# Normalised y of a fused state-space and feed-forward block: split token-major and transposed by DMA, the norm's scale and shift moved into the gate's weights and bias, y rebuilt by channel on GpSimd

## The reference

```
z0, x0, xBC, dt = split(layernorm(x) @ W_in.T)
xBC = silu(causal_conv4(xBC) + conv_b);  x, B, C = split(xBC)
h_t = exp(dt*A) h_(t-1) + dt * x_t B_t;  y_t = h_t C_t + D * x_t    (8 heads of 64 channels, 16 states)
y = layernorm(y) * ln_gamma + ln_beta                               (512 channels)
y = sigmoid(y @ W_gate.T + b_gate) * y
x = x + concat(silu(z0) * x0, y) @ W_out.T
h = layernorm(gelu(layernorm(x) @ tern(W_fc).T)) * ln_w + ln_b;  x = x + h @ tern(W_proj).T
```

## Time and profile before

| | |
|---|---|
| runs | 1303.48, 1304.63, 1305.02 us (median 1304.63) |
| profiled execution, its own time | 1306.39 us |
| its span, first to last instruction | 1304.6 us |
| mean granted TensorE clock | 0.962 |
| TensorE busy | 1150.3 us (88%), 8534 matmuls |
| VectorE (DVE) busy | 1061.3 us (81%), 2116 instructions |
| ScalarE (ACT) busy | 929.3 us (71%), 1500 instructions |
| GpSimd (POOL) busy | 348.3 us (27%), 388 instructions |
| DMA | 89.10 MB, queue of the kernel busy 30.5% of 16 engines' span |

### The profile page before, as it was taken

One profiled execution on the slowest core, in us unless ns is written; L12 is line 12 of the kernel. 1 busy time (PEld: TensorE's weight loads), 2 busy tenths in 40 slices (PEclk: granted clock), 3 DMA queues, 4 the chain that ended last, 5 costly groups with the idle time before them and its releaser, 6 DMA issues.

```text
span 1304.6 us, 22529 instructions
## 1 busy us (share of the span) xinstructions
PE 1150.3 (88%) x8534; PEld 732.5 (56%) x8534; DVE 1061.3 (81%) x2116; ACT 929.3 (71%) x1500; POOL 348.3 (27%) x388
## 2 busy tenths in 40 slices
PE   3575999999999999999999999899998989798875
PEld 1352556656575656656565756656565555555453
DVE  6888888888989889888889898889888786755543
ACT  5857586867778786867778785868677686666634
POOL 0011214141413214141413223142413213241410
PEclk9778999999999999999999999999999999999987
DMA  4620112232323424232323433233323221422344
GB/s 141 189 66 9 34 23 60 58 89 51 91 50 73 82 58 79 54 90 50 91 50 73 82 73 68 49 85 62 83 41 75 57 49 42 68 63 42 73 81 81
DMA packets 238971, 89.10 MB, mean 68 GB/s; under 512 B 207760, under 2 KB 235152, under 8 KB 238864
## 3 DMA queue, kind: packets, MB, share of 16 engines
q1 hardware_dynamic: 238864, 87.67, 30.5%
HBM read 24.32 MB, written 8.39 MB: 25 GB/s over the span
## 4 chain that ended last, share of the span: by engine, by line
PE 44%; DVE 23%; ACT 21%; DMA 7%; issue 4%; POOL 1%; SPq 0%; DVEq 0%
PE bank L166 22%; PE bank L140 22%; DMA hT<-hb 6%; DVE cv L144 3%; ACT L161 3%; ACT hb L141 3%; DVE hb L142 3%; DVE hn L144 3%; ACT cv L141 3%; ACT h L141 2%; ACT yT L141 2%; ACT EM L141 2%; ACT yhl L141 2%; DVE tg L144 2%; ACT xbuf L141 2%
## 5 line engine op out<-in xcount | busy, mean ns | idle before, releaser
L166 PE MATMUL bank<-xnT,win 128*128 128x512 f16 (+1 forms) x1040 | 265.1, 386 | 17.1 <-DMA xnT<-hb 16.9
L144 DVE SCALAR_TENSOR_TENSOR cv<-xbuf,cws,cv 128x512 f32<-128x512 f32 (+1 forms) x240 | 182.0, 759 | 10.3 <-ACT cv L141 3.5
L166 PE MATMUL bank<-yhl,wg 128*128 128x512 f16 x704 | 167.9, 388 | 21.6 <-DVE yhl L142 12.7
L166 PEld LDWEIGHTS bank<-xnT,win 128*128 128x128 f16 (+1 forms) x1040 | 102.2, 102 | 130.3 <-issue 26.6
L140 PE MATMUL bank<-wpj,hT 128*128 128x256 f16 x1040 | 133.2, 285 | 43.6 <-DMA hT<-hb 38.9
L140 PEld LDWEIGHTS bank<-wpj,hT 128*128 128x128 f16 x1040 | 102.6, 102 | 76.9 <-issue 21.6
L140 PE MATMUL bank<-wfc,x3T 128*128 128x512 f16 x512 | 130.4, 387 | 6.0 <-DMA x3T<-hb 5.9
L161 ACT ACT_TABLE_LOAD x95 | 121.9, 1283 | 13.4 <-PE bank L140 11.7
L166 PEld LDWEIGHTS bank<-yhl,wg 128*128 128x128 f16 x704 | 68.5, 99 | 108.4 <-ACT EM L141 12.5
L142 POOL TENSOR_TENSOR cat<-sz,cat 128x512 f16<-128x512 f32 x64 | 80.2, 1253 | 160.4 <-ACT cat L141 160.4
L141 ACT ACTIVATE h<-bank,rs 128x512 f32<-128x512 f32 x128 | 87.3, 684 | 48.7 <-PE bank L140 46.8
(11 more groups left out here) (131 smaller groups left out, 2363.2 us busy)
## 6 DMA issues: line engine op xcount, KB each, us to landing
x<-in_x SPq DMA_DIRECT2D x32, 512.0 KB, 4.1
out_y<-x SPq DMA_DIRECT2D x15, 512.0 KB, 2.9
crep<-cv SPq DMA_DIRECT2D x128, 32.0 KB, 1.9
hT<-hb SPq DMA_TRANSPOSE x128, 3.2
segR<-segL SPq DMA_DIRECT2D x64, 6.0 KB
caty<-in_wg SPq DMA_DIRECT2D x1, 1024.0 KB, 5.6
x<-in_wout SPq DMA_DIRECT2D x1, 1024.0 KB, 8.9
hT<-in_wfc SPq DMA_DIRECT2D x1, 1024.0 KB, 10.9
```

Source lines behind the costliest of these rows:

```text
L144: "scalar_tensor_tensor": lambda e: e.scalar_tensor_tensor(*args, **kw),
L166: self.queue.append(lambda e: e.matmul(*args, **kw))
```

## The change

The four channel groups of `yout` after "yn" go; a new generator `yturn` stands between `yout` and `gate`. It calls `hilo_T` twice per block, each time on two chunks (128 x 1024 values of `yT`, reordered from channel group, chunk to chunk, channel group), so `hb` has eight users per block and SP issues four more transposing DMAs. What is transposed is the normalised y without gamma and beta. Gamma is multiplied into the gate's weights by row (channel), and beta goes through the gate's matrix into the bias, in `prep_gate`. Since `yT` held the token-major values, y by channel is rebuilt: GpSimd adds high and low half of `yhl` into `yf`, ACT applies gamma and beta. `yhl` gets a chunk-major layout. `PLAN` has new due times in most tasks, the last entry of `SHIFT` goes from 14.8 to 12.6, and `AHEAD` from 5 to 6.

```diff
-AHEAD = 5
+AHEAD = 6
+    "yturn": (78, 78.5, 80.6, 80, 88, 83.1, 91.6, 91, 103.3, 93, 94, 94.9, 96, 97, 98, 99),
...
-        yhl = sb("yhl", [P, 2, 4, T], f16)
+        yhl = sb("yhl", [P, 2, NCH, 4, P], f16)
...
-        t_bg = V.do([ts], "tensor_scalar", bgh[:, :], sm("bg"), 0.5, None, ALU.mult)
+        t_lg = V.do([ts], "tensor_scalar", lg64[:, :], sm("lng"), SW, None, ALU.mult)
...
         def prep_gate():
-            yield Need(A, ("twg", 0))
-            a1 = A.do([dn["twg", 0]], "activation", wg[:, 0, :, :], wgs, ACT.Copy, scale=SW)
-            dn["wg", 0] = V.do([a1], "scalar_tensor_tensor", wg[:, 1, :, :].rearrange("p k n -> p (k n)"),
-                               wgs.rearrange("p k n -> p (k n)"), SW, wg[:, 0, :, :].rearrange("p k n -> p (k n)"),
-                               ALU.mult, ALU.subtract)
+            yield Need(PE, ("twg", 0), banks=1)
+            b, f = take()
+            PE.wait(f, dn["twg", 0], ts)
+            for g in range(4):
+                for k in range(4):
+                    m = PE.do([], "matmul", b[:, g:g + 1], wgs[:, k, g * P:(g + 1) * P], sm("lnb")[:, k:k + 1],
+                              start=(k == 0), stop=(k == 3))
+            v = V.do([m], "tensor_tensor", bgh[:, :], b[:, 0:4], sm("bg"), ALU.add)
+            give(b, v)
+            dn["bg", 0] = V.do([v], "tensor_scalar", bgh[:, :], bgh[:, :], 0.5, None, ALU.mult)
+            for k in range(4):
+                yield Need(A, ("twg", 0))
+                a1 = A.do([dn["twg", 0], t_lg], "activation", wg[:, 0, k, :], wgs[:, k, :], ACT.Identity,
+                          scale=lg64[:, k:k + 1])
+                v = V.do([a1], "scalar_tensor_tensor", wg[:, 1, k, :], wgs[:, k, :], lg64[:, k:k + 1],
+                         wg[:, 0, k, :], ALU.mult, ALU.subtract)
+            dn["wg", 0] = v
...
-        def hilo_T(a_waits, src, dst, sems, count, done, war):
+        def hilo_T(a_waits, src, dst, sems, count, done, war, grid=None):
+            (with grid, hb is seen as chunk, channel group, token)
...
+        def yturn(i):
+            for p in range(2):
+                yield from hilo_T([("yn", 4 * i + 2 * p), ("yn", 4 * i + 2 * p + 1)],
+                                  yT[:, :, 2 * p * P:2 * p * P + 2 * P].rearrange("p j (c t) -> p c j t", c=2),
+                                  [yhl[:, q, 2 * p:2 * p + 2, :, :].rearrange("p c k t -> p (c k) t") for q in range(2)],
+                                  s_y, 2 * i + p + 1, ("yhl", 2 * i + p), [("gate_read", i - 1)], (2, 4))
+            dn["y", i] = [dn["yhl", 2 * i], dn["yhl", 2 * i + 1]]
             for j in range(4):
-                yield Need(PE, ("yn", 4 * i + 3), ("gate_read", i - 1), banks=1)
-                b, f = take()
-                PE.wait(f, dn["yn", 4 * i + 3])
-                for c in range(NCH):
-                    m = PE.do([], "transpose", b[:, c * P:(c + 1) * P], yT[:, j, chunk(c)], ident)
-                dn["yt_mm", 4 * i + j] = m
-                yield Need(A, ("yt_mm", 4 * i + j))
-                a = A.do([m], "activation", yf[:, j, :], b[:, :], ACT.Identity,
-                         scale=sm("lng")[:, j:j + 1], bias=sm("lnb")[:, j:j + 1])
-                give(b, a)
-                a = A.do([a, old("gate_read", i - 1)], "activation", yhl[:, 0, j, :], yf[:, j, :], ACT.Copy)
-                dn["yhi", 4 * i + j] = a
-                yield Need(V, ("yhi", 4 * i + j))
-                v = V.do([a, old("gate_read", i - 1)], "tensor_tensor", yhl[:, 1, j, :], yf[:, j, :], yhl[:, 0, j, :],
-                         ALU.subtract)
-            dn["y", i] = v
+                yield Need(G, ("y", i))
+                v = G.do([dn["y", i], dn["split", ("yhl", 2 * i + 1)]], "tensor_tensor",
+                         yf[:, j, :].rearrange("p (c t) -> p c t", c=NCH), yhl[:, 0, :, j, :], yhl[:, 1, :, j, :], ALU.add)
+                dn["ysum", 4 * i + j] = v
+                yield Need(A, ("ysum", 4 * i + j))
+                dn["yf", 4 * i + j] = A.do([v], "activation", yf[:, j, :], yf[:, j, :], ACT.Identity,
+                                           scale=sm("lng")[:, j:j + 1], bias=sm("lnb")[:, j:j + 1])
...
         def gate(i):
-                m = three(..., lambda q, k: yhl[:, q, k, :], ...)
+                m = three(..., lambda q, k: yhl[:, q, :, k, :], ...)
-                yield Need(V, ("tanh", at))
+                yield Need(V, ("tanh", at), ("yf", at))
```

More of the change, by code:

```diff
@@ L29 @@
 PLAN = {
[L30 to L33, removed]
[4 rows of a table removed]
-    "gate": (108.4, 112.0, 122.6, 122.9, 120.0, 117.1, 125.3, 125.7, 125.1, 130.0, 131.7, 130.6, 130.8, 134.4,
-        136.7, 135.8),
-    "inputs": (-20.7, -4.7, 1.6, 2.0, 2.5, 5.7, 3.0, 8.0),
@@ L41 @@
[L41 to L57, removed]
+    "conv": (-104.9, -85.0, -83.9, -81.3, -76.8, -79.2, -72.5, -67.3, -64.7, -60.8, -57.6, -59.5, -55.1, -49.6,
+        -46.3, -45.0, -44.2, -41.9),
@@ new lines @@
+    "decay": (-18.9, -18.9, -17.8, -5.9, -5.4, -1.4, 9.5, 11.0, -4.0, 9.5),
+    "dt_chain": (-68.4, -65.6, -38.9, -33.3, -28.6, -23.4, -17.5, -21.0, -21.5, -19.2),
[4 rows of a table added]
+    "gate": (108.4, 112.0, 122.6, 122.9, 120.0, 117.1, 125.3, 125.7, 125.1, 132.8, 131.7, 131.1, 130.8, 134.1,
+        132.4, 135.8),
+    "inputs": (-20.7, 4.0, 1.6, 9.2, 2.5, 5.7, 3.2, 8.0),
+    "ln1": (-118.6, -97.9, -95.5, -88.6, -98.4, -95.6),
+    "ln3": (193.2, 194.2),
+    "mix": (7.2, 10.1, 26.6, 29.9, 20.6, 36.9, 17.4, 34.2, 34.5, 37.9, 42.7, 47.7),
@@ new lines @@
+    "out": (103.7, 142.3, 158.1, 162.8, 182.2, 194.5, 191.7, 188.7, 192.7),
+    "proj": (228.6, 233.3, 231.3, 241.7, 239.2, 242.4, 249.7, 253.4),
+    "silu": (-41.4, -25.5, -18.0, -19.4),
+    "skip": (46.2, 45.6, 48.3, 52.8, 112.9, 108.2, 113.4, 111.5, 117.3, 117.2, 115.9, 116.1, 113.8, 94.8, 96.1,
+        98.6, 99.0, 124.1, 123.5, 122.8),
+    "states": (20.7, 17.7, 11.5),
+    "turn3": (195.3, 188.0, 192.8, 197.1),
+    "wffn": (102.9, 112.0, 115.9, 117.4, 123.8, 117.6, 129.8, 128.0, 123.1, 130.8, 132.2),
@@ L58 @@
+    "wgate": (67.1, 70, 70.5, 70.3, 71.5),
+    "win": (8.6, 15.6, 20.0),
+    "wout": (77.8, 109.4),
+    "yout": (32.2, 32.1, 49.5, 80.4, 78.6, 79.3, 71.6, 66.3, 68.4, 68.1, 69.6, 72.7, 77.6, 76.6, 77.3, 86.3,
+        86.6, 88.3, 90.8, 86.4, 92.9, 96.1),
+    "yturn": (78, 78.5, 80.6, 80, 88, 83.1, 91.6, 91, 103.3, 93, 94, 94.9, 96, 97, 98, 99),
 }
 PERIOD = 76.4
-SHIFT = (0.0, 0.0, 0.0, 0.0, 0.0, 0.0, 0.0, 0.0, 0.0, 0.0, 0.0, 0.0, 0.0, -0.4, -2.4, 14.8)
-AHEAD = 5
+SHIFT = (0.0, 0.0, 0.0, 0.0, 0.0, 0.0, 0.0, 0.0, 0.0, 0.0, 0.0, 0.0, 0.0, -0.4, -2.4, 12.6)
@@ L219, in build @@
         s_xt = [sem(f"s_xt{q}") for q in range(2)]
+        s_y = [sem(f"s_y{q}") for q in range(2)]
         s_x3 = [sem(f"s_x3{q}") for q in range(2)]
@@ L243, in build @@
         bgh = sb("bgh", [P, 4])
+        lg64 = sb("lg64", [P, 4])
         cws = sb("cws", [P, 5, 4])
@@ L494, in hilo_T @@
             ready = [old(*k) for k in war]
-            a = A.do([dn[k] for k in a_waits] + [dn["hb_free0", 0]], "activation", hb[:, 0, :], src, ACT.Copy)
+            hi, lo = (hb[:, q, :].rearrange("p (c k t) -> p c k t", c=grid[0], k=grid[1]) if grid else hb[:, q, :]
+                      for q in range(2))
+            a = A.do([dn[k] for k in a_waits] + [dn["hb_free0", 0]], "activation", hi, src, ACT.Copy)
             dn["hb", done] = a
@@ L499, in hilo_T @@
             yield Need(V, ("hb", done), ("hb_free1", 0))
-            v = V.do([a, dn["hb_free1", 0]], "tensor_tensor", hb[:, 1, :], src, hb[:, 0, :], ALU.subtract)
+            v = V.do([a, dn["hb_free1", 0]], "tensor_tensor", lo, src, hi, ALU.subtract)
             dn["split", done] = v
@@ L849, in gate @@
                 b, f = take()
-                m = three(b[:, :], lambda p, k: wg[:, p, k, g * P:(g + 1) * P], lambda q, k: yhl[:, q, k, :],
+                m = three(b[:, :], lambda p, k: wg[:, p, k, g * P:(g + 1) * P], lambda q, k: yhl[:, q, :, k, :],
                           [f, dn["y", i], dn["wg", 0]], range(4))
@@ L854, in gate @@
                 tt = tg[:, g % 2, :]
-                dn["tanh", at] = a = A.do([m, old("glo", at - 2), t_bg], "activation", tt, b[:, :],
+                dn["tanh", at] = a = A.do([m, old("glo", at - 2), dn["bg", 0]], "activation", tt, b[:, :],
                                           ACT.Tanh, scale=0.5 / SW, bias=bgh[:, g:g + 1])
                 give(b, a)
-                yield Need(V, ("tanh", at))
-                dn["yf_read", at] = V.do([a, dn["y", i]], "scalar_tensor_tensor", tt, tt, 1.0, yf[:, g, :],
+                yield Need(V, ("tanh", at), ("yf", at))
+                dn["yf_read", at] = V.do([a, dn["yf", at]], "scalar_tensor_tensor", tt, tt, 1.0, yf[:, g, :],
                                          ALU.add, ALU.mult)
@@ L991, in proj @@
             dn["done", i] = True
-        TASKS = (ln1, conv, silu, dt_chain, inputs, decay, states, mix, yout, gate, skip, out, turn3, ln3, fc, proj)
```

(1 more changed line is left out.)

## The result

The changed kernel takes 1347.6 us (median of 4 runs, 1343.96 to 1349.79), the kernel before 1304.11: a ratio of 1.033, interval 1.0306 to 1.0354. The forecast was 1285 us, the range ended at 1319. The whole working came out wrong in sign, so the question is which of its terms.

The account below looks back on a forecast made before the run. TensorE was taken as the bound, DVE close behind. The period of 67.4 + 3.1 + 0.7 = 71.2 us saves 1.46, times 14 20.4 us; 1306.4 - 20.4 + 1.0, less 1.8, gives 1285 us, range 1261 to 1319.

Parts of the forecast that it names:

- So TensorE bounds the regular part: Regular part: TensorE, busy 69.54 of 72.66 us per period, sets the time, with DVE close behind at 64.99.
- those 2.1 us per period: Transposes of `yT` back, 16 per block in four batches of 0.53 us: their removal takes 2.1 us off TensorE.
- busier engine plus 3.1 us idle: The period's sum: busier engine's 67.4 us, plus 3.1 us it stood above that engine before, plus 0.7 us, gives 71.2.
- GpSimd's hold on DVE: Four new additions per block hold up DVE, 0.6 us each, 2.4 us per period, bringing DVE to 67.3 us.
- the 0.7 us of mutual waiting: Regular part: TensorE and DVE about equally full wait for each other, 0.7 us per period, from 0 to 1.2.
- The rival of the port: Each GpSimd addition stops DVE for its whole length, 1.2 us: period 73.5 us, total time 1318 us, chance 0.24.
- Its last sentence: If DVE also kept its 9% idle of the y stretch: period 76.6 us, total time over 1350; given little chance.
- the latency of y: From last "yn" to gate: the new path's 12 us fits into the 20 us there, so it costs nothing.
- the DMAs: SP issues four more per block, with other DMAs queued behind: new waits taken as 0, from 0 to 1.5 us per period.
- the buffer rival: Two more `hb` users per block delay `hT` or `x3T`, taking back the 1.46 us per period: 1304 us, chance 0.12.
- The order: Retimed plan and one more open block: no cost in the sum, only a possible gain in the first rival.
- the first rival: More won: additions cost DVE only 0.31 us each, 30 us less; with a third of TensorE's idle closed, 1262 us; chance 0.14.

Follow-up runs that it names:

- b7: Kernel before, own queues, with 12 of the 16 transposes back per block left out: 1309.0 us, ratio 1.0065.
- b2: Kernel before, own queues, with four GpSimd additions of y's halves per block added, result read by nobody: 1336.5 us, ratio 1.0272.
- a1: Changed kernel, same queue order, GpSimd's four additions per block one column wide, ACT making by-channel y from the high halves: 1319.7 us, ratio 1.0127.
- a2: Changed kernel, same queue order, with y's halves written to the bytes of `tg` instead of `hb`: 1346.7 us, ratio 1.0342.
- a3: Changed kernel, same queue order, with both narrow additions and y's halves in the bytes of `tg`: 1322.1 us, ratio 1.0147.
- a6: As a1, but ACT and DVE write y's halves straight into `yhl`, without the four transposing DMAs per block: 1326.1 us, ratio 1.0168.

## Why the prediction was wrong

**The failed step is the first: "So TensorE bounds the regular part".** It was read from 69.54 busy us of 72.66. Removing three quarters of those 2.1 us per period, 1.6 us (b7), gained nothing, so no run shows any of the term of 2.1 us * 14 = 29 us (some 5 us of it at most, if the lower clock of b7 is set aside). The signs were there before: in the stretch from 745 us on DVE was 91% busy and ACT 89%, and the gate, which reads what the transposes feed, was held back 1.06 us by ACT's `EM`. The page of the kernel before has the plainest one, the chain of work that ended last, as shares of the span:

```profile
PE 44%; DVE 23%; ACT 21%; DMA 7%; issue 4%; POOL 1%; SPq 0%; DVEq 0%
```

TensorE is busy 88% of the span, but the chain runs through it for 44%, and through DVE and ACT together for as much. TensorE's high share there was the share of an engine that is fed by two others without a gap. The sum "busier engine plus 3.1 us idle" has no place for work whose end nobody waits for.

**GpSimd's hold on DVE.** The price was somewhat low: 0.6 us per addition was taken. DVE's busy time shows 0.75 in b2, in the changed kernel, 46 us more with 0.1 us per period less of its own, (46 + 1.6) / 64 = 0.74, and against a1 54 / 64 = 0.85. What was wrong is what it costs: DVE with the hold, 67.3 us, stayed under TensorE's 67.4 in the sum, so the hold came in only as the 0.7 us of mutual waiting, 10 us in the run. It cost some 26 us in the changed kernel, and 34 in b2 for 48 us of hold. The rival of the port named the mechanism, but with full length as its condition ("it decides from about 1.0 us per addition"); it decided at 0.75, because the TensorE gain against which it was weighed did not exist. Its 1318 us were too low too. Its last sentence says that the period would be 76.6 us if DVE also kept its idle share of the stretch, and gives that little. The period is 76.6 us, partly by luck, since DVE has 68.66 us in it and not 69.7; but DVE's busy share of the period did stay, 89.4% before and 89.6% after.

**The buffer `hb`, the latency of y, the DMAs.** Counted at nothing; a2 and a3 bear that out for the buffer. For the DMAs a6 shows no gain, at a lower clock, and leaves a cost of some us open. The sign named for the buffer rival, TensorE waiting for `hT` by much over 38.9 us, did come (75.1), from another cause: a sign that two mechanisms share tells nothing between them.

**The order.** The new plan was counted at nothing, and in the first rival as a possible gain of a third of TensorE's idle time. It is the largest lever that was touched: 30 to 50 us for the kernel before.

**TensorE's clock** was not in the sum. At 322 us transposes filled a pause, and the kernel before stayed at 1.00 where b7 went to 0.50. By the estimate above the lower clock took back some 12 us of the 25 us of work that b7 leaves out.

**What stays open.** Of the 43 us, some 26 are the additions. The other 18 are the new order together with the new steps of y; they weren't separated, since every other order tried costs more than 18 us by itself. The mean clock of a1's runs is 0.952, as low as b7's, which by the same sum is up to 15 us of TensorE's work done late; what lowered it there is not shown. That the lower clock makes up b7's loss is a sum over mean clocks and busy times, not an experiment.

## What to carry to other kernels

An engine that is busy 95% of a period need not bound it: before booking the removal of its work, look at how much of the chain that ended last is on it, and at whether the few instructions right behind that work then wait for another engine. A GpSimd addition of 1.2 us that reads SBUF, put beside a dense DVE, cost DVE 0.75 to 0.85 us here and the run 0.4 to 0.5; if DVE can do the same in less time, leave it there. In a kernel with a tuned static order, weigh a change against what a reordering alone costs (here 30 us and more), and change work and order in separate runs.

## What the runs showed of the hardware

GpSimd's memsets (0.5 us each) beside DVE's two-input instructions cost nothing where additions (1.2 us and more) cost 34 us over 64 instructions. TensorE's granted clock falls to 0.50 in the middle of a run in which it is 87% busy: in b7 behind two stretches of 2 us with 1.31 and 1.25 us of work, after which the five `xnT` matmuls took 2.31 us instead of 1.25.
